# A four-stage vision tower on one core: the embedding loop's root chain, key rows and weight layout changed, and the last MLP's bias moved into its product

## Time and profile before

| | us |
|---|---|
| median of 3 runs | 2718.76 (2715.95 to 2720.96) |
| profiled execution, its own time | 2716.97 |
| its span | 2714.9 |
| embedding loop, start to last statistics | 0 to 445 |
| MLP A | 450.8 to some 840 |
| attention B | 845 to some 2430 |
| last MLP | 2469 to the end |

### The profile page before, as it was taken

The page is one execution under the profiler, slowest core; times in us unless marked ns, Lnnn a source line. Parts: engine busy times, 40 slices in busy tenths (PEclk is TensorE's granted clock), DMA queues, the critical chain, the costliest instruction groups (busy, mean ns, idle before and its releaser), DMA issues. The chain is left out here.

```text
span 2714.9 us, 83446 instructions
## 1 busy us (share of the span) xinstructions
PE 2498.4 (92%) x27448; PEld 2120.4 (78%) x27448; DVE 2254.3 (83%) x5864; ACT 2089.7 (77%) x6198; POOL 1232.4 (45%) x1805
## 2 busy tenths in 40 slices
PE   5878886999997999999999999999999999996776
PEld 5767774888885888888888888888888888884554
DVE  6767876777775888888888888888888888887998
ACT  4867895555554888888888888888888888886998
POOL 6867882333331343434343334334433443344664
PEclk9988996999998999999999999999999999997999
DMA  6422330000001333333233333333333333320111
GB/s 202 134 81 84 103 90 1 1 0 0 0 0 37 73 81 68 74 72 80 67 73 75 79 68 70 77 77 70 67 80 74 73 67 80 72 63 14 40 43 46
DMA packets 181704, 173.54 MB, mean 64 GB/s; under 512 B 19063, under 2 KB 180289, under 8 KB 181378
## 3 DMA queue, kind: packets, MB, share of 16 engines
q1 hardware_dynamic: 181634, 172.64, 26.2%
HBM read 46.68 MB, written 9.68 MB: 21 GB/s over the span
## 5 line engine op out<-in xcount | busy, mean ns | idle before, releaser
L1323 POOL TENSOR_TENSOR b_pr<-b_pr,b_rinv 128x394 f32<-128x394 f32 (+1 forms) x768 | 626.5, 843 | 1006.8 <-DVE b_rinv L1281 1006.8
L1218 ACT ACTIVATE b_pr<-b_banks,b_nmx 128x197 f32<-128x197 f32 (+1 forms) x1536 | 625.8, 424 | 27.5 <-DVE b_nmx L1275 25.3
L1189 ACT ACTIVATE b_pt<-b_bank_t 128x394 f16<-128x394 f32 (+1 forms) x768 | 337.8, 494 | 202.7 <-PE b_bank_t L1154 202.5
L1275 DVE TENSOR_REDUCE b_nmx<-b_banks 128x2 f32<-128x394 f32 (+1 forms) x768 | 397.3, 558 | 65.5 <-PE b_banks L1144 57.3
L1246 DVE TENSOR_TENSOR b_pt<-b_bank_t,b_pt 128x394 f16<-128x394 f32 (+1 forms) x768 | 395.9, 556 | 18.2 <-ACT b_pt L1189 18.2
L1128 PE MATMUL b_banks<-b_xt,wqkv 128*128 128x197 f16 x3840 | 374.0, 249 | 4.4 <-DVE b_xt L1246 2.2
L1154 PE MATMUL b_bank_t<-ident,b_pr 128*128 128x128 f32 (+3 forms) x3072 | 341.8, 253 | 3.1 <-DVE b_pt L1246 3.0
L1128 PEld LDWEIGHTS b_banks<-b_xt,wqkv 128*128 128x128 f16 x3840 | 321.0, 98 | 25.5 <-issue 18.8
L1144 PE MATMUL b_banks<-b_kst,b_qst 128*128 128x197 f16 (+1 forms) x3072 | 326.7, 248 | 7.4 <-ACT b_pr L1218 4.9
L1154 PEld LDWEIGHTS b_bank_t<-ident,b_pr 128*128 128x128 f32 (+3 forms) x3072 | 282.1, 142 | 42.9 <-issue 35.4
L1218 ACT ACTIVATION_READ_ACCUMULATOR b_pr<-b_banks,b_nmx 128x1 f32 (+1 forms) x1536 | 315.0, 205 | 0.0
(11 more groups left out here) (206 smaller groups left out, 4665.0 us busy)
## 6 DMA issues: line engine op xcount, KB each, us to landing
b_qst<-b_qk SPq DMA_DIRECT2D x512, 147.8 KB, 2.5
b_kst<-b_qk SPq DMA_DIRECT2D x512, 73.9 KB, 2.3
patches<-in_x SPq DMA_DIRECT2D x64, 588.0 KB, 4.3
out<-z_res SPq DMA_DIRECT2D x32, 192.0 KB
out<-z_res SPq DMA_DIRECT2D x32, 103.5 KB
h<-in_wqkv SPq DMA_DIRECT2D x2, 1152.0 KB, 6.5
h<-in_w SPq DMA_DIRECT2D x2, 576.0 KB, 7.0
h<-in_fc SPq DMA_DIRECT2D x1, 768.0 KB
```

Of the source, the lines that this page charges most:

```text
L1189: return nc.scalar.activation(dst, src, ACT.Copy)
L1218: last = nc.scalar.activation(pr[n % 3][0:ROWS[c], c, e, :], banks[0:ROWS[c], c, e * SEQ:(e + 1) * SEQ], ACT.Exp, bias=nmx[n % 2][0:ROWS[c ...
L1275: v.reduce_max(nmx[n % 2][0:ROWS[c], c, :], banks[0:ROWS[c], c, 0:2 * SEQ].rearrange("p (e t) -> p e t", e=2), AX.X, negate=True).then_inc ...
L1323: last = nc.gpsimd.tensor_tensor(p, p, inv, ALU.mult)
```

## The change

The embedding loop's orders are written anew; every pair goes through its jobs up to one round later than before. POOL's root chain runs once for two pairs, on 128x8 numbers, in the odd pair's round, behind all six pieces of `l`. The key rows are added on DVE from the normalised rows (`u`), and ACT no longer does it. `w_proj` and `b_fc` are laid out turned on the host, so PE turns nothing; their factors are made in six columns (`gc`), the upper half is rounded by ACT (`high_fp`), the lower half formed by DVE (`low_fp`). In the last MLP the bias is divided by the scale, split in three bf16 rows (`split_bias`), and added by one more matmul for each product; POOL now adds `h`, and DVE's `add_stream` and POOL's `add_bias` are gone.

```diff
-    PE_ORDER = "x^^ t^^^ E1 m^^^ s^^ j^^^^ E0'".split()
-    ACT_ORDER = ("e^^^^ g^^^^^ h0 u^^^ k^^^ n^^ h1 x^^").split()
-    DVE_ORDER = ("x^^ p^^^ f^^^^^ o^^^^ t^^^ a0 s^^^^^ b0 a1 b1 i^^^ r m^^").split()
-    POOL_ORDER = ("l00 l01 l02 l10 l11 q1^ q2^ q3^ q4^ q5^ l12 q6^ q7^ q8^ q9^ q10^ "
+    PE_ORDER = "E1 t^^^^ x^^^ j^^^^^ m^^^^ s^^^ E0'".split()
+    ACT_ORDER = ("h1 k^^^^ n^^^ x^^^ h0' e^^^^ g^^^^^").split()
+    DVE_ORDER = ("f^^^^^^ m^^^^ s^^^^^^ a0 x^^^ p^^^^ u^^^^ o^^^^^ t^^^^ b0 a1 b1 i^^^^ r").split()
+    POOL_ORDER = ("l00 l01 l02 l10 l11 l12 q1^ q2^ q3^ q4^ q5^ q6^ q7^ q8^ q9^ q10^ "
                  "q11^ q12^ q13^ q14^ q15^").split()
...
                     n = int(s[1:])
+                    if b == 0:
+                        return
+                    moment = lambda k: mv[:, :, :, k].rearrange("p b j -> p (b j)")
                     if n == 1:
                         pool.wait_ge(aggregated, p + 1)
-                        last = g.tensor_tensor(var[b][:], mv[b][:, :, 1], eps[:], ALU.add)
+                        last = g.tensor_tensor(var[:], moment(1), eps[:], ALU.add)
...
+                def high_fp():
+                    act.wait_ge(masked, 2)
+                    copy(S["fp"][:, 0], r_fp[:]).then_inc(weights_hi, 1)
...
-                    elif kind == "u":
-                        act.wait_ge(xn_made, p + 1)
-                        act.wait_ge(norm[LAST_NORM], p + 1)
-                        for m in range(2):
-                            for c, rows in ((0, slice(NK1, P)), (1, slice(0, TAIL))):
-                                x, j = h[rows, 2 * p + m, c, :], 2 * m + c
-                                last = nc.scalar.activation(x, x, ACT.Identity, bias=my[b][rows, j:j + 1], scale=y1[b][rows, j:j + 1])
-                        last.then_inc(keys_added, 1)
...
+                def hidden_columns():
+                    for j, r in enumerate(RATIO_CHOICES):
+                        for i, e in enumerate(EMBED_CHOICES):
+                            whole, rest = divmod(r * e, P)
+                            column = alpha[:, 3 + j:4 + j]
+                            if whole:
+                                last = v.tensor_scalar(gc[:, i, 0:whole], gc[:, i, 0:whole], column, None, ALU.add)
+                            if rest:
+                                part = gc[0:rest, i, whole:whole + 1]
+                                last = v.tensor_scalar(part, part, column[0:rest], None, ALU.add)
+                        then(last)
...
+                def mask_fp():
+                    for i, e in enumerate(EMBED_CHOICES):
+                        begin = EMBED_CHOICES[i - 1] if i else 0
+                        factor = gc[:, i, :].unsqueeze(2).to_broadcast([P, HC, e - begin])
+                        last = v.tensor_tensor(r_fp[:, :, begin:e], r_fp[:, :, begin:e], factor, ALU.mult)
+                    last.then_inc(masked, 1)
...
+                def low_fp():
+                    dve.wait_ge(weights_hi, 2)
+                    then(v.tensor_tensor(S["fp"][:, 1], r_fp[:], S["fp"][:, 0], ALU.subtract))
...
+                def split_bias():
+                    b, rows, picked = S["q2_bias"], S["bias_rows"], S["picked"]
+                    then(v.reciprocal(c1b[:], S["q2_scale"][:]))
+                    then(v.tensor_tensor(b[:], b[:], c1b[:], ALU.mult))
+                    then(v.tensor_copy(rows[:], b[:]))
+                    then(v.tensor_tensor(b[:], b[:], rows[:], ALU.subtract))
...
+                    elif kind == "u":
+                        dve.wait_ge(xn_made, p + 1)
+                        for c, rows in ((0, slice(NK1, P)), (1, slice(0, TAIL))):
+                            keys = h[rows, bass.ds(2 * p, 2), c, :]
+                            last = v.tensor_tensor(keys, keys, xn[b][rows, :, c, :], ALU.add)
+                        last.then_inc(keys_added, 1)
...
+                first_slot = {2: coefficient(1), 17: split_bias, 3: coefficient_sum(0), 4: hidden_columns, 13: invert_rows(1), 15: invert_rows(3), 16: divide_second}
+                second_slot = {1: coefficient(0), 2: coefficient(2), 3: coefficient_sum(1), 4: mask_fc, 5: mask_fc_bias, 6: mask_fp, 7: mask_fp_bias,
+                               8: low_fc(0), 9: low_fc(1), 10: low_fp, 11: means, 12: scales, 13: invert_rows(0), 14: invert_rows(2),
+                               15: divide_first, 16: quantise(0), 17: quantise(1), 18: sum_second, 19: low_wo}
...
-                pipeline(dve, turns, [(clip_hidden(0, 1), 1), (finish, -1), (clip_hidden(2), 1), (add_stream, -1), (take_turned_x, 2),
-                                      (clip_hidden(3, 4, 5), 1), (quantise, 3)])
+                pipeline(dve, turns, [(clip_hidden(0, 1), 1), (finish, -1), (clip_hidden(2), 1), (take_turned_x, 2),
+                                      (clip_hidden(3, 4, 5), 1), (quantise, 3)])
+
+            @block.gpsimd
+            def _(pool):
                 def add_stream(u, b):
-                    dve.wait_ge(scaled[b], u + 1)
-                    dve.wait_ge(bias_added[b], u + 1)
+                    pool.wait_ge(scaled[b], u + 1)
                     i = image(u, b, 0)
                     for c in range(2):
                         r = res[b][0:ROWS[c], :, c, :]
-                        last = v.tensor_tensor(r, h[0:ROWS[c], bass.ds(i, 2), c, :], r, ALU.add)
+                        last = nc.gpsimd.tensor_tensor(r, h[0:ROWS[c], bass.ds(i, 2), c, :], r, ALU.add)
                     last.then_inc(h_done[b], 1)
...
                             for f in range(HC):
-                                last = t.matmul(y, low_half[b][:, f, lo:lo + ROWS[c]], S["q2"][:, f, :], start=False, stop=(f == HC - 1))
+                                t.matmul(y, low_half[b][:, f, lo:lo + ROWS[c]], S["q2"][:, f, :], start=False, stop=False)
+                            last = t.matmul(y, S["picked"][:, 0:ROWS[c]], S["bias_rows"][:], start=False, stop=True)
```

174 lines of the change are left out of this document (64 added, 110 removed).

## The result

| | before | changed |
|---|---|---|
| median | 2719.7 (2715.6 to 2721.8, 8 runs) | 2727.2 (2723.0 to 2730.8, 8 runs) |
| ratio, 95% interval | | 1.003 (1.0019 to 1.0041) |
| span of the profiled execution | 2714.9 | 2725.7 |

The forecast was 2671 us, with a range of 2642 to 2704. The time lies outside, on the other side of no change. Rival 4 came nearest: slower, with the loop through DVE and PE deciding.

The account below looks back on a forecast made before the run. Bounds were POOL's full beat and weight-turning stalls in the embedding loop, and DVE with a two-beat loop in the last MLP. Terms -38 and -9 gave -47 from 2717.0, 2670; adjusted to the median, 2671 us, range 2642 to 2704.

Parts of the forecast that it names:

- Rival 4: Embedding loop: the loop through `u` and PE decides, beats 11.5 without weights, 14.0 with them; +21, 2740 us; chance 0.07.
- Pairs 9 to 15: Embedding loop: the three weight-turning stalls go, DVE is late next; 71.5 us against 97.5, -26, the largest term.
- Pairs 15 to 23: Embedding loop: DVE's 92.7 us plus waits, 12.1 a beat; 97 us against 95.5, +1.5.
- the beat after: Embedding loop: DVE takes over from POOL as the bound, 10.6 us a beat without weight work; loop through PE 9.8 to 10.5.
- Pairs 0 to 9: Embedding loop: beat of 10.8 us with waits, now 12.4; 97.5 us against 111.2, -13.5.
- Pairs 23 to 31: Embedding loop without weight work: 8 beats of 10.6, 85 us against 88.9, -4.
- `u`'s price: Key rows on DVE: two instructions of 0.7 us, 1.4 a pair, between bounds of 1.1 and 2.5.
- a sign of being wrong: `u` on DVE: expected at 0.6 to 0.8 us an instruction; above 1 us would count against the forecast.
- Root chain: Embedding loop, POOL: once for two pairs, POOL falls to 8.2 us a pair; loss priced 0, at most 1.3 every second beat.
- Drain: End of embedding loop: one beat more without patch work, bounds 0 and 11 us; PE's share without tokens 3.3, so +4.
- Last MLP: Final stage: beat falls from 7.2 to 6.9 us over 31 pairs, net -9, bounds -20 and +3.
- loop of two beats: Last MLP: scaling, down product, Gelus, clips and quantise close in 14.44 us, falling to 13.8, 6.9 a beat.

Follow-up runs that it names:

- e2: Kernel before with the new last MLP and weights laid out turned on the host; old orders, chain per pair, `u` on ACT: 2678.8 us, ratio 0.9861.
- e7: e2 with the key rows (`u`) added on DVE behind `t` instead of on ACT: 2698.5 us, ratio 0.9920.
- e13: Changed kernel with the root chain once for each pair, on four columns with two sets of tiles: 2728.2 us, ratio 1.0037.
- e11: e2 with every job behind the root one round deeper, chain still per pair: 2693.3 us, ratio 0.9905.
- e8: e11 with the root chain shared, once for two pairs, `u` on ACT: 2708.6 us, ratio 0.9962.
- e9: Changed kernel with `u` back on ACT, behind `g`: 2730.3 us, ratio 1.0039.
- e4: Changed kernel with DVE's weight work moved from behind `a0` and `a1` to behind `b0` and `b1`: 2712.5 us, ratio 0.9988.
- e12: e9 with the weight work moved behind `b0` and `b1`: 2715.3 us, ratio 0.9986.
- e6: Changed kernel with `u` left out, a one-element memset in its place (a measure only): 2682.9 us, ratio 0.9864.
- e15: e2 with the weight work moved behind `b0` and `b1`: 2682.8 us, ratio 0.9873.

## Why the prediction was wrong, by its own steps

Two paths of smaller edits lead from e2 to the changed kernel. By the differences:

| path | steps, us |
|---|---|
| 1 | e2, `u` on DVE +18.6, e7, new orders +29.8, e13, shared chain -2.3, changed |
| 2 | e2, deeper +12.8, e11, shared chain +15.9, e8, new orders +21.1, e9, `u` on DVE -3.7, changed |

Both sum to 46. Path 1's new orders hold the deeper drain too (10.9 from e7 to e13); without it they are 19, and 21 on path 2. Of these the weight work's place is up to 12 to 15 (e4, e12). The two paths disagree on the chain and on `u`. Sharing costs 15.9 in the old orders and nothing behind the new ones. `u` costs 18.6 in the old orders; path 2's -3.7 is no price of `u`, since the step also takes away e9's wait. Prices taken in one order do not carry to another.

- **Pairs 9 to 15, the stall of the weight turning.** -26 was forecast for the whole change, with 8.4 us for `u` in DVE's sum. The same sum without `u` gives 62.8 us, 34.7 less than before; without `u` on DVE e2 takes 72.0 and e6 71.2. So the layout brought 25.5 and not 34.7, and that e2 comes near -26 is chance. `u` and the new orders then took 11 us back (82.9).
- **Pairs 15 to 23: the step that failed, the bound of "the beat after".** It took DVE's busy time plus 0.5 a beat for waits and came to 97. DVE's sum was forecast at 92.7 and is 101.7; but 116.0 - 101.7 = 14.3 us are waits, 1.8 a beat. The prediction wrote down the loop (tokens, `a0`, `x`, `p`, `u`, `o`, `t`, then PE) and priced it at 9.8 to 10.5, without the weight work behind `a0`, which is inside it, and with PE's work at the length it had before. e4, e12 and e15 show the first: 12 and 15 in the new orders, nothing in the old. By the profiles of this stretch `u` costs 17.1 us (e6) where 11.2 was priced, and the weight work's place 7.2 (e4); the two overlap. For the second there was no term: PE's busy time grew by 16 us (94.73 for 78.77) at a clock of 0.81 for 0.95. Rival 4 said it with the right price (+16.5 here, +20.5 measured) and was given 0.07, since "half the weight work stands behind `a1`, off this loop". The half behind `a0` was enough.
- **`split_bias`** was 3.5 us of DVE and takes 7.8 (247.77 to 255.6), all of it in that loop. One of its casts in the changed kernel, beside POOL's pieces, and in e4, with POOL idle (duration min/median/max in ns, start):
```profile
L656 DVE CAST bias_rows<-q_bias x1: 871/871/871, 252.6 to 252.6; 64x192 bf16<-64x192 f32 x1
```
```profile
L656 DVE CAST bias_rows<-q_bias x1: 257/257/257, 247.5 to 247.5; 64x192 bf16<-64x192 f32 x1
```
- **Pairs 0 to 9.** 10.8 a beat was forecast and 13.1 came out, 20.3 us in all and as large a miss as in pairs 15 to 23. Neither `u` (115.3 us in e6), nor the place of the weight work (114.6 in e4), nor the shared chain (121.2 in e13) brings it near the 97.5 forecast, and e2 with the old orders has 112.1. PE waits for POOL's pieces there, once for 7.9 us, and its clock is 0.81. The least of the new orders is 108.9 (e12, with `u` on ACT and the weight work behind `b0` and `b1`), of the old ones 108.0 (e15). What keeps it there stays open.
- **Pairs 23 to 31.** 10.6 was forecast, 11.2 measured. e6 shows the beat without `u` at 9.7. `u` costs 1.5 a beat here, near the 1.4 priced, but on top of a beat of 9.7 of which DVE fills 7.8 without it.
- **`u`'s price.** 1.8 us a pair (57.9 in 32 pairs) for a predicted 1.4, with a median of 1.15 us an instruction, above the 1 us named as a sign of being wrong. In e7, where DVE has time, it cost 18.6 us, in part through POOL. The prediction's bounds had only DVE's side: that DVE's instruction also holds up POOL's chain, and through it ACT, was not in the sum.
- **Root chain.** Priced at 0 to 1.3 in every second beat as a loss, with POOL's 3.8 - 2.5 as gain (the 2.5 counts gaps, the 3.8 does not; half of 3.8 is 1.9). The gain is worth nothing in the new orders (e13). The price is met in the old orders (e8: 15.9/16 = 1.0 in every second beat).
- **Drain.** +4 was read as PE's share without tokens. A drain beat is not PE's sum but one trip round PE, DVE and ACT. Timeline of the changed kernel:
```profile
444.40 0.28 DVE L722 TENSOR_TENSOR prs<-pr,prs 128x133 f16<-128x133 f32 x1
...
444.74 0.32 PE L498 MATMUL bank_p<-ident,prs 128*69 128x128 f16 x1 [2.81 <-DVE prs L722]
...
447.47 1.54 ACT L365 ACTIVATE xt<-bank_x 96x788 f16<-96x788 f16 x2 [2.85 <-PE bank_x L480]
...
453.41 0.32 PE L498 MATMUL bank_p<-ident,prs 128*69 128x128 f16 x1 [2.81 <-DVE prs L722]
```
  From transposition to transposition 453.41 - 444.74 = 8.67 us, at a granted clock of 0.50, and e11 shows that the depth alone costs 10.8.
- **Last MLP.** Right in direction, -14.2 for -9, but the bound is another than the forecast loop of two beats. Lines of the changed kernel in 2530 to 2602 us:
```profile
L1456 ACT ACTIVATE z_act<-z_bank_h,q_bias,q_scale 128x394 f32<-128x394 f32 x65 | 43.9, 675 | 1.8 <-PE z_bank_h L1488 1.7
L1446 ACT ACTIVATE z_hid<-z_act,inv_a 128x394 f32<-128x394 f32 x64 | 39.7, 621 | 0.0
L1399 DVE TENSOR_SCALAR z_act<-z_act,q_hi,q_lo 128x394 f32<-128x394 f32 x64 | 36.3, 581 | 4.4 <-ACT z_act L1456 4.2
...
L1419 POOL TENSOR_TENSOR z_res<-h,z_res 69x384 f32<-69x384 f32 (+1 forms) x21 | 22.6, 1093 | 46.3 <-DVE z_res L1406 46.3
```
  POOL's sum takes 2 x 1093 ns a pair, not the 5.0 us taken from the earlier trace rows. The clips are longer than before (581 ns in the mean, 525 before), 0.3 us a beat, inside the 0.5 allowed. ACT is busy 70.19 of 72 us (60.43 of 65 before), so its six Gelus and six roundings set the beat, and not the loop of two beats, for which 6.9 had been worked out. It is (2554.34 - 2520.60)/5 = 6.75 us:
```profile
2520.60 1.01 DVE L1406 TENSOR_TENSOR z_res<-z_bank_y,q_scale 128x384 f32<-128x384 f32 x2
...
2554.34 1.01 DVE L1406 TENSOR_TENSOR z_res<-z_bank_y,q_scale 128x384 f32<-128x384 f32 x2
```
  31 x (7.2 - 6.75) = 14, where 6.9 had been forecast.

In the total the embedding loop came out 63 us above the forecast (+25.4 for -38), the last MLP 5 below.
